# Attention steps over two head pairs in a transformer sandwich kernel on one Trainium2 core

## The reference, cut to what matters

```python
# x: (16, 256, 128); Wq, Wk, Wv: (16 heads, 128, 64); Wo: (1024, 128)
def attn(x, Wq, Wk, Wv, Wo, gamma, beta):
    q = einsum('bsd,hde->bhse', x, Wq); k, v likewise
    scores = einsum('bhse,bhte->bhst', q, k)
    scores = where(causal, scores / sqrt(64), -inf)
    attn = softmax(scores, axis=-1)
    out = einsum('bhst,bhte->bhse', attn, v)
    y = x + heads(out) @ Wo
    return layernorm(y, eps=1e-3) * gamma + beta
x = x + layernorm(attn(layernorm(x), ...))
x = x + layernorm(moe(layernorm(x), router_w, w1, w2))   # 8 experts, top 2, gelu, width 512
```

## Time and profile before

| | |
|---|---|
| median of three runs | 774.43 us |
| profiled execution, its own time | 777.19 us |
| span of the profile | 775.4 us |
| PE busy | 720.7 us (93%) |
| DVE busy | 592.5 us (76%) |
| ACT busy | 525.4 us (68%) |
| POOL busy | 275.4 us (36%) |

### The profile page before, as it was taken

One profiled execution on the slowest core, in us unless ns is written; L12 is line 12 of the kernel. 1 busy time (PEld: TensorE's weight loads), 2 busy tenths in 40 slices (PEclk: granted clock), 3 DMA queues, 4 the chain that ended last, 5 costly groups with the idle time before them and its releaser, 6 DMA issues.

```text
span 775.4 us, 18459 instructions
## 1 busy us (share of the span) xinstructions
PE 720.7 (93%) x5954; PEld 606.0 (78%) x5955; DVE 592.5 (76%) x2298; ACT 525.4 (68%) x1751; POOL 275.4 (36%) x404
## 2 busy tenths in 40 slices
PE   4899999999999999999999999999987899999954
PEld 3787778888888888878878788888766889999921
DVE  4668898989898888889898888889895765444316
ACT  4677777777777777777777777777763555555505
POOL 3005354141323323131313323232312677555534
PEclk9999999999999999999999999999997999999978
DMA  8350000000000000000000000000002144322156
GB/s 182 117 118 8 9 8 23 8 22 15 22 12 20 19 11 23 8 23 13 17 16 22 16 15 22 8 23 1 24 13 59 53 108 118 81 73 82 45 167 177
DMA packets 53947, 34.94 MB, mean 45 GB/s; under 512 B 10624, under 2 KB 50560, under 8 KB 53856
## 3 DMA queue, kind: packets, MB, share of 16 engines
q1 hardware_dynamic: 48224, 23.81, 11.9%
q0 software_dynamic: 4544, 9.45, 3.4%
q10 hardware_dynamic: 1088, 0.54, 0.3%
HBM read 20.22 MB, written 13.56 MB: 44 GB/s over the span
## 4 chain that ended last, share of the span: by engine, by line
PE 81%; DVE 8%; ACT 4%; issue 3%; DMA 2%; POOL 1%; DVEq 1%; POOLq 0%; SPq 0%; ACTq 0%
PE PT1O L420 12%; PE SC L406 10%; PE A L599 8%; PE A L426 6%; PE M L385 6%; PE M L387 5%; PE M L386 5%; PE SC L412 5%; PE SC L409 3%; PE PT L433 3%; PE PT L434 3%; PE PT1O L437 3%; PE SC L385 2%; PE SC L387 2%; PE SC L386 2%
## 5 line engine op out<-in xcount | busy, mean ns | idle before, releaser
L1092 ACT ACTIVATE qk<-M 128x512 f32<-128x512 f32 x128 | 76.5, 597 | 139.9 <-PE M L387 139.9
L1098 ACT ACTIVATE prob<-SC,nmax 128x256 f32<-128x256 f32 x256 | 125.6, 491 | 0.0
L420 PE MATMUL PT1O<-pT,v_sb 128*64 128x256 f32 (+1 forms) x1024 | 112.2, 339 | 12.2 <-issue 7.4
L420 PEld LDWEIGHTS PT1O<-pT,v_sb 128*64 128x64 f32 x1024 | 65.7, 136 | 55.0 <-issue 22.4
L708 DVE TENSOR_SCALAR prob<-prob,rden 128x256 f32<-128x256 f32 x256 | 101.7, 397 | 9.1
L1096 ACT ACTIVATE prob<-SC,nmax 128x128 f32<-128x128 f32 x256 | 96.6, 377 | 0.0
L1318 POOL DMA_INDIRECT expert_rows<-v_sb,got x78 | 77.8, 997 | 48.1 <-ACT v_sb L1188 31.0
L406 PE MATMUL SC<-qk 64*128 64x256 f32 x512 | 91.0, 432 | 0.8 <-ACT qk L1092 0.8
L1310 POOL DMA_INDIRECT sent_rows<-rec,slot x64 | 64.0, 1001 | 72.4 <-DVE slot L868 54.4
L702 DVE TENSOR_REDUCE nmax<-SC 128x2 f32<-128x512 f32 x128 | 87.1, 680 | 0.0
L385 PE MATMUL M<-xt_hi,wqk_hi 128*128 128x256 f32 x256 | 83.9, 328 | 1.3 <-DVE xt_lo L697 1.3
(11 more groups left out here) (183 smaller groups left out, 1780.6 us busy)
## 6 DMA issues: line engine op xcount, KB each, us to landing
got<-sent_rows SPq DMA_DIRECT2D x39, 132.0 KB, 2.3
w_in<-expert_rows SPq DMA_DIRECT2D x16, 256.0 KB, 4.1
x_in<-L_attn_x SPq DMA_DIRECT2D x16, 128.0 KB, 2.1
w_in<-L_ffn_w SPq DMA_DIRECT2D x1, 2048.0 KB, 12.1
x_res<-L_attn_x SPq DMA_DIRECT2D x16, 128.0 KB, 2.1
w_sb<-L_ffn_w SPq DMA_DIRECT2D x8, 256.0 KB, 4.5
out<-y_out SPq DMA_DIRECT2D x8, 256.0 KB, 2.4
sent_rows<-pad_rec SPq DMA_DIRECT2D x11, 132.0 KB, 4.3
```

The source lines that it names most:

```text
L420: last = mm(O[k * E:(k + 1) * E, cols], v_sb[:, t, h * E:(h + 1) * E], src[:, k, :], start=(t == 0), stop=(t == 1), skip_group_check=True)
L1098: a.activation(prob[:, par, k, P:3 * P], SC[par][:, k, LATE_Q], ACT.Exp, bias=nmax[:, par, k:k + 1], accum_out=den[:, par, k:k + 1]).then_ ...
```

## The change

A step takes two head pairs. A batch has four steps `u`, and pairs `2k` and `2k+1` (with `k = 4b + u`) belong to one. Tiles `qk`, `pT0`, `pT1`, `hT` are doubled, `prob` has four slots, and the value sums of two pairs use the whole bank `PT1O`. The two heads of a pair are divided by one reciprocal and two `tensor_tensor` multiplications with the reciprocals broadcast. The work on other batches is put at other places of the steps, the dispatch and the sends of a batch come one batch later, and the statistics of a new batch one step earlier. PE now does, in a step: `qk_proj`, six transposes, `w_o` of two pairs, `qk_proj`, six transposes, `v_proj` (in every step), value sums of two pairs, scores of two pairs, masks of two pairs.

```diff
-        qk = sb("qk", [P, 2, S])
+        qk = sb("qk", [P, 2, 2, S])
-        prob = sb("prob", [P, 2, 2, 3 * P])
+        prob = sb("prob", [P, 4, 2, 3, P])
...
+            def masks(par):
+                for k in range(2):
                     last = mm(SC[par][:, k, P:S + P], ident_bf[:], mask[:]..., start=False, stop=True)
                 last.then_inc(s_mm, 1)
...
+            def pv_two(c):
+                pv(c, 0)
+                pv(c + 1, 1).then_inc(pv_mm, 1)
...
+            def step(b, u):                       # PE
+                k = STEPS * b + u
+                p = 2 * k
+                c = 2 * u
+                if u == 1 and there(b, 2):
+                    pe.wait_ge(pt0_sb, p - 2)
+                    rows_transpose(PT0, b - 2)
+                if more:
+                    if k >= 1:
+                        pe.wait_ge(v_done, 4 * b + 1 + u)
+                    qk_proj((c + 2) % NP)
+                if k >= 1:
+                    pe.wait_ge(nrm, p - 1)
+                    ...
+                    p_transpose(p - 2)
+                if u == 0 and there(b, 3):
+                    rows_before(b - 3, before_out(True), False)
+                if u == 1 and there(b, 2):
+                    if more:
+                        pe.wait_ge(qk_sb, p + 3)
+                    logits(b - 2)
+                if u == 2 and there(b, -1):
+                    pe.wait_ge(qk_sb, p + 3)
+                    x_transpose(b + 1)
+                if k >= 2:
+                    pe.wait_ge(o_sb, k - 1)
+                    ...
+                    w_o((c - 4) % NP)             # two pairs
+                if more:
+                    pe.wait_ge(qk_sb, p + 3)
+                    if u == 1 and there(b, 2):
+                        pe.wait_ge(sem("lg_done"), b - 1)
+                    if u == 2 and there(b, -1):
+                        pe.wait_ge(sem("xt_st"), b + 2)
+                    qk_proj((c + 3) % NP)
+                if k >= 1:
+                    pe.wait_ge(nrm, p)
+                    pe.wait_ge(pt0_sb, p - 1)
+                    pe.wait_ge(pt1_sb, p - 1)
+                    p_transpose(p - 1)
+                if turn:
+                    if more:
+                        pe.wait_ge(qk_sb, p + 4)
+                    v_proj(turn[0], turn[1])
+                if k >= 1:
+                    pe.wait_ge(pt0_sb, p)
+                    pe.wait_ge(pt1_sb, p)
+                    pv_two((c - 2) % NP)
+                if more:
+                    pe.wait_ge(exp_done, p + 1)
+                    scores(0)
+                    pe.wait_ge(exp_done, p + 2)
+                    scores(1)
+                    masks(0)
+                    masks(1)
...
+            def normalise_pair(p):                # DVE
+                slot, par = p % 4, p % 2
+                dve.wait_ge(exp_done, p + 1)
+                v.reciprocal(rden[:, par], den[:, par]).then_inc(rc, 1)
+                dve.wait_ge(rc, p + 1)
+                v.tensor_tensor(prob[:, slot, :, 1:3, :], prob[:, slot, :, 1:3, :],
+                                rden[:, par, 0, :].unsqueeze(2).unsqueeze(3).broadcast_to([P, 2, 2, P]), ALU.mult)
+                v.tensor_tensor(prob[:, slot, :, 0, :], prob[:, slot, :, 0, :],
+                                rden[:, par, 1, :].unsqueeze(2).broadcast_to([P, 2, P]), ALU.mult).then_inc(nrm, 1)
...
+            def step(b, u):                       # DVE
+                maxima(p)
+                if not first:
+                    pT1_copy(p - 2)
+                    normalise_pair(p - 1)
+                if u == 1 and there(b, 2):
+                    router(b - 2, 3)
+                maxima(p + 1)
+                ...                               # router 0 | attended | first_norm, router 5 | finish, router 6
+                if not first:
+                    pT1_copy(p - 1)
+                normalise_pair(p)
+                ...                               # router 1, counts, dispatch | attention_stats, router 4, x_normalise
+                                                  # | x_split, second_stats | x_stats
...
+            def step(b, u):                       # ACT
+                if u == 1 and there(b, 2):
+                    xfT_copy(PT0, b - 2)
+                if more:
+                    qk_copy(p + 2)
+                exps_early(p, 0)
+                exps_late(p, 0)
+                if u == 2 and there(b, -1):
+                    xt_copy(b + 1)
+                if k >= 1:
+                    pT0_copy(p - 2)
+                if u == 1 and there(b, 2):
+                    router_exp(b - 2)
+                exps_late(p, 1)
+                if more:
+                    qk_copy(p + 3)
+                exps_early(p, 1).then_inc(exp_done, 1)
+                if k >= 1:
+                    pT0_copy(p - 1)
+                exps_early(p + 1, 0)
+                exps_late(p + 1, 0)
+                exps_early(p + 1, 1)
+                exps_late(p + 1, 1).then_inc(exp_done, 1)
+                if turn:
+                    v_copy(turn[2], turn[0], turn[1])
+                if k >= 1:
+                    o_copy(k)
+                if u == 2 and there(b, 2):
+                    records(b - 2)
```

More of the change, by code:

```diff
@@ L192, in sandwich_kernel @@
         mx = sem("mx")
-        exp_done = [sem(f"exp_done{k}") for k in range(2)]
+        exp_done = sem("exp_done")
         rc, nrm = sem("rc"), sem("nrm")
@@ L428, in w_o @@
[L428 to L438, removed]
+                for par in range(2):
+                    for t in range(T):
+                        last = mm(A[:, t * D:(t + 1) * D], hT[:, par, t * P:(t + 1) * P], wo_sb[:, c + par, :],
+                                  start=(c == 0 and par == 0 and t == 0), stop=(c + par == NP - 1),
+                                  skip_group_check=True)
@@ new lines, in rows_transpose, with logits @@
+            def rows_transpose(dst, r):
+                pe.wait_ge(sem("xf_done"), r + 1)
+                for t in range(T):
+                    last = nc.tensor.transpose(dst[:, t * P:(t + 1) * P], xf[:, t, :], ident[:])
+                last.then_inc(sem("xfT_mm"), 1)
+            def logits(r):
+                pe.wait_ge(sem("xfT_sb"), r + 1)
+                for t in range(T):
+                    last = mm(M[:, t * NE:(t + 1) * NE], xfT[:, t * P:(t + 1) * P], rw_sb[:],
+                              start=(t == 0), stop=True, skip_group_check=True)
+                last.then_inc(sem("logit_mm"), 1)
@@ new lines, in batch @@
+            def batch(b):
+                if not there(b):
+                    for j in range(NP):
+                        closing(b, j)
+                        epilogue_tile(b, j)
+                    return
+                for u in range(STEPS):
+                    step(b, u)
+                if is_last(b):
+                    end = NP * B
+                    pe.wait_ge(nrm, end - 1)
+                    pe.wait_ge(pt0_sb, end - 2)
+                    pe.wait_ge(o_sb, STEPS * B - 1)
+                    p_transpose(end - 2)
+                    first_rows()
+                    pe.wait_ge(nrm, end)
+                    pe.wait_ge(pt0_sb, end - 1)
+                    pe.wait_ge(pt1_sb, end - 1)
+                    p_transpose(end - 1)
+                    pe.wait_ge(exp_done, end)
+                    up(0, 0)
@@ new lines, in batch @@
+            def batch(b):
+                if there(b):
+                    for u in range(STEPS):
+                        step(b, u)
+                    if is_last(b):
+                        normalise_pair(NP * B - 1)
+                        pT1_copy(NP * B - 2)
+                        first_splits()
+                    return
+                for j in range(NP):
+                    if b == B and j == 0:
+                        pT1_copy(NP * B - 1)
+                        counts_copy(B - 3, True)
+                    if b == B:
```

479 lines of the change are left out of this document (228 added, 251 removed).

## The result

The changed kernel took 790.18 us (median of 4 runs, 786.75 to 791.13). The kernel before, timed beside it, took 774.22 (4 runs, 772.11 to 776.05): a ratio of 1.0182 (95% interval 1.0161 to 1.0203). The forecast was 759.0 with a range of 741 to 778, so direction, size and range were all wrong. The profiled execution of the change took 790.08 us with a span of 788.3.

What follows compares the result with a forecast made beforehand. PE was taken to bound the kernel (34.71 of 35.14 us per batch). Steps -14.6, start -3.8 and end +3 made -15.4: profiled 777.19 to 761.8, median 759, range 741 to 778 (8 in 10).

Steps and rivals of the forecast that it cites:

- (1) The shape changes: PE's value sums, scores and masks: one round of array-shape changes for two pairs instead of two, -0.47 us per step.
- Rival D: PE's late starts belong to each group of value sums or scores, so grouping saves nothing: 789 us, chance 0.05.
- (2) The division: DVE's division of both heads at once: about 1.1 us against 1.3, long operation 0.69, off the path if in time.
- Rival C in its first form: DVE's division falls behind, broadcast operand at half rate: 0.6 us more per step, 797 us; both forms together 0.13.
- (3) The walk of one step: All engines' queues through a two-pair step: 8.07 us, about 0.2 of the saving lost as the value projection waits for M.
- (4) The other work: Work on other batches within the steps: +0.3, +1.1, +0.5, +0.2 us for u=0 to 3, sum 2.1; batch 34.4.
- break-even at 0.25 us per step: A delay of 0.25 us per step, from a division 0.45 late, would cancel the forecast gain of 15.4 us.
- rival C's milder form: DVE runs over from step to step by 0.4 us: 25 us more, 784 us; both forms together 0.13.
- (5) Start and end: Before pair 1's masks -3.8 us; at the end, weight copies ahead of a division, +3 (bounds 0 and +6).
- A (no waits): ACT and DVE finish earlier than assumed, M is free in time: batch 33.2 us, kernel 740 us, chance 0.16.
- B: All given back: other work's waits 3 us per batch rather than 2.1, end costs 6: 774 us, chance 0.08.

Runs made afterwards that it cites:

- masks_apart: The changed kernel with the two pairs' scores and masks taken apart again (scores, masks, scores, masks): 802.78 us, ratio 1.0358.
- u23_later: The changed kernel with DVE's router part 5 (u=2) and part 6 (u=3) moved behind the division: 759.64 us, ratio 0.9783; in a later comparison 790.72, 0.9938.
- pool_small: The changed kernel, order kept, with POOL's two operations on z2 cut to one column of each tile: 769.74 us, ratio 0.9922.
- u2_later: The changed kernel with only DVE's router part 5 in u=2 moved behind the division: 769.31 us, ratio 0.9921.

## Why the prediction was wrong, by its own steps

**(1) The shape changes: right.** The scores of two pairs in the changed kernel:

```profile
292.10 0.70 PE L403 MATMUL SC<-qk 64*128 64x256 f32 x4
292.64 0.39 PE L406 MATMUL SC<-qk 64*128 64x128 f32 x4
292.86 0.60 PE L403 MATMUL SC<-qk 64*128 64x256 f32 x4
293.29 0.39 PE L406 MATMUL SC<-qk 64*128 64x128 f32 x4
```

The second pair follows the first after 0.22, the streaming time of two groups of 128, with no late start; its groups of 256 take 0.43, twice 0.21, where the first pair's take 0.54. `masks_apart` gives the price from the other side, 0.3 for one change more and back. Rival D is out.

**(2) The division: size right, place half right.** 0.69 was taken for the long operation, 692 ns is the mean between 300 and 560 us (705 over the whole kernel). In the new order it is off the path but in u=1 (0.2 per batch, in favour of both heads at once). That this could be said of the edit by itself was wrong: in the old order it costs 1.1 per batch. Rival C in its first form, a division at half rate, is out.

**(3) The walk of one step: right.** 8.07 forecast; 8.10 to 8.20 in the steps without other work (batches 0 and 1), 8.15 in u=3 of `u23_later`. The value projection starts 0.30 after the last transpose instead of 0.11, so the 0.2 of waiting for `M` was there too.

**(4) The other work: the step that failed.** The terms were +0.3, +1.1, +0.5 and +0.2, for steps of 8.37, 9.17, 8.57 and 8.27. Measured: 8.34, 9.38, 9.98 and 8.83. The errors are 0.0, +0.2, +1.4 and +0.6, together +2.1 per batch; over the 12 steady batches 26 us of the 28 by which the profiled time was missed (790.1 against 761.8). Terms of u=0 and u=1 were right or near. In u=2 I counted the wait for ACT and no operation of DVE at all, in u=3 only the normalisation, and nowhere that POOL could hold one. So u=1 was not the longest step, as forecast, but u=2. Taking the router's operations out of the way gives 8.69 and 8.15 (`u23_later`), against 8.57 and 8.27: the walk was right for what it contained.

What it lacked is this. Until the change, POOL's operations on z2 ran beside DVE operations that they did not hold, and the addition of x held a division for which PE was not waiting (the transposes at 297.62 in the kernel before follow the projection without a gap). The new order puts `first_norm`, which releases POOL, directly ahead of the router's part 5, and `finish` directly ahead of part 6, and both ahead of the copy of `pT1`. So the same hold now falls into the only stretch of DVE's queue on which PE waits. The prediction had said that "anything that holds DVE ahead of that division adds to it" and put the break-even at 0.25 us per step; the hold came to 1.6 per batch (1.07 in u=2 by `pool_small`, 0.55 in u=3 by the row of the cast), 0.4 per step. The other 0.5 of the 2.1 is about the place of the router's operations (0.2 in u=2, 0.1 in u=3) and the 0.2 of u=1. That the whole miss, 26 us, is close to the 25 of rival C's milder form is chance: C had DVE overrunning by its own work, did not name this cause, and had 0.13.

Two steps lost more than the steady ones. In u=2 of batch 2 POOL's weight splitting holds two more of DVE's router operations, and PE waits 2.04 us instead of 1.24 for the value sums; in u=2 of batch 15 it waits 1.95. Behind these two waits the granted clock was low (0.54 from 106.3 to 110.0, and 0.62 from 583.5 to 588.0, mostly the lower level of 1.2 GHz), and the same 16 value matmuls took 2.74 and 2.11 us instead of 1.52:

```profile
583.54 2.11 PE L420 MATMUL PT1O<-pT,v_sb 128*64 128x256 f32 x16 [1.95 <-issue]
```

The two steps, 12.42 and 12.24, are 4.7 us above twice 9.98.

The rows for it lay in the trace of the kernel before, unread. DVE, and POOL beside it:

```profile
295.81 0.85 DVE L708 TENSOR_SCALAR prob<-prob,rden 128x256 f32<-128x256 f32 x1
296.58 0.27 DVE L710 TENSOR_SCALAR prob<-prob,rden 128x128 f32<-128x128 f32 x1
296.78 0.15 DVE L706 RECIPROCAL rden<-den 128x2 f32<-128x2 f32 x1
296.96 0.35 DVE L708 TENSOR_SCALAR prob<-prob,rden 128x256 f32<-128x256 f32 x1
```
```profile
295.78 0.73 POOL L1301 TENSOR_TENSOR x<-x_res,z 128x256 f32<-128x256 f32 x1 [4.32 <-DVE z L680]
```

One operation, 0.85 and then 0.35, and POOL's addition starts 0.03 ahead of the long one; it is so in every steady batch. The prediction used the mean of that line, 398 ns, in which this is gone.

**(5) Start and end.** Start -4.8, forecast -3.8. End +5.1, forecast +3 with bounds 0 and +6: inside. Moving the weight copies did not measurably shorten it, so the reason given for it (copies ahead of a division) is not shown.

Rivals A (no waits) and B (34.4 becomes 35.3, 774) did not happen, though `u2_later` is B's batch to 0.1, by another cause. B's sum has a slip that changes nothing: its end of 6 and start of -3.8 make 2.2 and not 0, so 774 should be 775.

## What to carry to other kernels

When an order is changed, walk DVE's and POOL's queues side by side: here POOL's two-tensor operations of 256 columns held DVE's casts, scalar and two-tensor operations on SBUF until they ended (0.72 to 0.75 us for 2 or 16 elements). Don't issue the operation that releases POOL directly ahead of such DVE work when the critical engine waits behind it; let the critical copy go first. And before a mean from the profile enters a sum, look at the longest single row of its line: a hold shows there and nowhere else.

## What the runs showed of the hardware

- The hold has nothing to do with the size of what is held: 16 elements take 0.17 to 0.18 alone and 0.75 beside POOL's 0.73; two of 16, 0.26 and 0.81; a cast of 2 elements, 0.17 and 0.72. It goes both ways (POOL 0.72 to 1.16).
- Not every operation is held. The copy of `pT1`, which reads PSUM, took 0.41 at 52.20 in the changed kernel, inside a two-tensor operation of POOL (51.99 to 52.72). A reciprocal of 2 values by DVE kept its 0.17 beside POOL's multiplication at 286.19 in the kernel before, too.
- Nor does every operation of POOL hold, also of those on two tensors. DVE's cast at 290.80 and comparison at 291.05 (shown above, 0.18 and 0.26) lie inside this one of the same kernel, 0.70 long on 2 elements:

```profile
290.76 0.70 POOL L1253 TENSOR_TENSOR rstd_z<-ve_z,half 128x2 f32<-128x2 f32 x1
```

- Changing the array's shape costs PE some 0.1 to 0.2 us each time, from two sides: 0.47 per round in the earlier trace rows, 0.3 for one more change and back.
- The same program's u=1 (`u23_later`) takes 9.4 us in one comparison and 10.0 to 10.8 in another, while its other steps stay within 0.03; unexplained.
